# Another written order of the first and last steps of a four-layer graph-attention kernel, with 25 extra matmuls in the last batch

## The reference, cut to what matters

```
h = relu(layernorm(x)); x = x + L0(h)   # 4 heads of 64: softmax over adj of leaky(s_i + s_j), times h W; elu
h = relu(layernorm(x)); x = x + L1(h)   # MLP 256->512, full attention (no mask), elu + residual,
                                        # MLP 512->256, masked attention (W_hand), elu + residual, relu
h = relu(layernorm(x)); x = x + L2(h)   # masked attention with self loops (W2), elu
h = relu(layernorm(x)); x = x + L3(h)   # masked attention (W3), relu
```

## Time and profile before

| | |
|---|---|
| median of 3 runs (lowest, highest) | 3086.91 us (3084.91, 3088.44) |
| the profiled execution | 3088.44 us, of which its span is 3086.6 us |
| PE busy | 3027.8 us (98%) |
| DVE busy, ACT busy | 2453.4 us (79%), 2321.4 us (75%) |
| mean granted clock of TensorE | 0.996 of full speed (2.4 GHz) |
| chain that ended last | PE 82%, ACT 9%, DVE 7% |

### The profile page before, as it was taken

One profiled execution on the slowest core, in us unless ns is written; L12 is line 12 of the kernel. 1 busy time (PEld: TensorE's weight loads), 2 busy tenths in 40 slices (PEclk: granted clock), 3 DMA queues, 4 the chain that ended last, 5 costly groups with the idle time before them and its releaser, 6 DMA issues.

```text
span 3086.6 us, 58782 instructions
## 1 busy us (share of the span) xinstructions
PE 3027.8 (98%) x21528; PEld 2830.1 (92%) x21528; DVE 2453.4 (79%) x7049; ACT 2321.4 (75%) x6303; POOL 205.2 (7%) x410
## 2 busy tenths in 40 slices
PE   8999999999999999999999999999999999999998
PEld 7899999999999999999999999999999998999987
DVE  6878787887887888878878888888778787787866
ACT  6677777777778777778787787777787777877776
POOL 2000000000000000000000000000000000000000
PEclk9999999999999999999999999999999999999998
DMA  2000000000000000000000000000000000000000
GB/s 76 1 22 1 15 15 15 15 1 15 15 15 15 15 1 15 15 15 15 2 14 15 15 15 15 1 15 15 15 15 8 8 15 15 15 15 1 1 1 28
DMA packets 16336, 41.54 MB, mean 13 GB/s; under 512 B 5297, under 2 KB 6833, under 8 KB 16049
## 3 DMA queue, kind: packets, MB, share of 16 engines
q1 hardware_dynamic: 16048, 37.77, 3.5%
HBM read 20.99 MB, written 16.78 MB: 12 GB/s over the span
## 4 chain that ended last, share of the span: by engine, by line
PE 82%; ACT 9%; DVE 7%; issue 1%; POOL 1%; SPq 0%; DMA 0%; DVEq 0%; ACTq 0%
PE bank L516 45%; PE bank L585 14%; PE bank L620 14%; ACT Z L1044 4%; PE bank L573 4%; PE bank L537 2%; DVE R L792 2%; PE bank L671 2%; PE bank L561 1%; DVE x L1009 1%; DVE Z L1006 1%; ACT Z L1196 1%; ACT Z L1202 1%; ACT Z L1191 1%; ACT Z L1021 1%
## 5 line engine op out<-in xcount | busy, mean ns | idle before, releaser
L585 PE MATMUL bank<-hw,R 128*128 128x257 f32 x3072 | 707.4, 383 | 0.5 <-DVE R L792 0.5
L585 PEld LDWEIGHTS bank<-hw,R 128*128 128x128 f32 x3072 | 569.0, 191 | 75.5 <-ACT hw L1082 1.5
L620 PEld LDWEIGHTS bank<-hw,R 128*128 128x128 f32 x4096 | 490.9, 192 | 5.5 <-DVE hw L825 1.2
L620 PE MATMUL bank<-hw,R 128*128 128x65 f32 x4096 | 494.8, 270 | 0.8 <-DVE R L792 0.8
L792 DVE SCALAR_TENSOR_TENSOR R<-bank,E,mask_ne 128x512 f32<-128x512 f32 x640 | 450.5, 743 | 13.4 <-PE bank L573 12.5
L1044 ACT ACTIVATE Z<-x,nm,rs 128x256 f32<-128x256 f32 x512 | 283.2, 593 | 52.3 <-DVE x L1009 32.2
L1247 POOL TENSOR_TENSOR rs<-ve,mhalf 128x4 f32<-128x4 f32 x128 | 134.5, 1051 | 2825.7 <-DVE ve L744 2159.2
L516 PE MATMUL bank<-wfc_hi,oThi 128*128 128x256 f32 (+1 forms) x1024 | 302.0, 295 | 2.1 <-DVE oTlo L871 1.9
L516 PE MATMUL bank<-wfc_hi,oTlo 128*128 128x256 f32 (+1 forms) x1024 | 289.7, 283 | 0.0
L516 PE MATMUL bank<-wfc_lo,oThi 128*128 128x256 f32 (+1 forms) x1024 | 289.7, 283 | 0.0
L1067 ACT COPY Z<-bank 128x258 f32<-128x258 f32 (+1 forms) x512 | 183.1, 369 | 93.3 <-PE bank L516 93.0
(11 more groups left out here) (262 smaller groups left out, 8353.9 us busy)
## 6 DMA issues: line engine op xcount, KB each, us to landing
x<-in_x_dram SPq DMA_DIRECT2D x32, 512.0 KB, 3.4
out_dram<-x SPq DMA_DIRECT2D x32, 512.0 KB, 2.6
R<-in_adj_dram SPq DMA_DIRECT2D x2, 512.0 KB, 7.3
Z<-in_L_gnn_mlp_w_dram SPq DMA_DIRECT2D x2, 512.0 KB, 5.4
O<-in_L_gnn_W_fc_dram SPq DMA_DIRECT2D x1, 1024.0 KB, 6.7
R<-in_L_gnn_W_dram SPq DMA_DIRECT2D x1, 256.0 KB, 3.7
R<-in_L_gnn_W_hand_dram SPq DMA_DIRECT2D x1, 256.0 KB, 6.7
rowt<-in_L_gnn_W_dram SPq DMA_DIRECT2D x1, 256.0 KB, 4.7
```

The lines of the kernel that those rows point to most:

```text
L585: ins = e.matmul(bk[:, 0:257], P[:, j, i * 128:(i + 1) * 128], hw[:, j, 0:257], start=(j == 0), stop=(j == NBLK - 1))
L620: ins = e.matmul(bk[:, i * 66:i * 66 + 65], P[:, (4 * h + j) % PTILES, i * 128:(i + 1) * 128], hv[:, j, h, 0:65], start=(j == 0 and i == 0 ...
```

## The change

All ten start and end strings of `TURNS` but SP's start are written anew; the cycle strings stay, and so does the number of steps that each batch has behind it at the end of the start. `warm` gets a batch number, and in `turn(2)` and `turn(3)` of the last batch (31) it issues 10 and 15 matmuls of 512 columns ahead of the transposes, into the bank that these then overwrite.

```
-            def warm(bk, n):
-                if b == 0:
+            def warm(bk, n, only=0):
+                if b == only:
                     w.wait_ge(*at("hTlo", b, 0, 1))
                     for _ in range(n):
                         e.matmul(bk[:, :], W0["hi"][:, 0, 0:128], hT[s]["hi"][:, 0, :], start=True, stop=True)
...
                     bk = bank_of(b, f"hT{l}", k)
+                    if k == 0 and l > 1:
+                        warm(bk, (10, 15)[l - 2], B - 1)
                     for n in range(NBLK):
```

The strings, of which one line of PE's end stands here:

```
-         "0000011112112000000111101010001000011110011101001001111010100100000"),
+         "1000110000011000000010111010000000110000000000000000000000000000000"),
```

More of the change, by code:

```diff
@@ L69 @@
     "pe": (
-        ("wwww00ww0000000w00000ww00001w10w0000ww0000w1www111ww00ww00001000011w000w000w111100102000000000121001"
-         "1111002010000011111000000020202001100000112111211020100001102120100110002210101121111112122210102120"
-         "00211100211211102222110111110001001011011"),
+        ("wwww00w00000w000000w000ww0ww00ww000ww0w0w0w001www1w1w100w0000110100010000100121111000000000000100111"
+         "1100011000001111100000002000000101001112122211210012000101012101102002020200121112111111122201012100"
+         "00211210112111202222011111111000010001111"),
@@ L73 @@
         ("2221100111010010101102201122221020102110022222021211011110110111221100022112212101111020000121111112"
          "122212221111"),
[L75 to L79, removed]
-         "0000011112112000000111101010001000011110011101001001111010100100000"),
+        ("5554343444433344343455335555445345454455535353454444444443334343535445355334455434444435333544444544"
+         "5545545544344434422333322323232443244434343324234322444424333333342223332323342242324443344323333324"
+         "2224333433334443434334332332311222211122121332332332321132123231313133222223221222112112331212113323"
+         "2323212222131113222322223332323322221122200111100011010221022122112102112022220002201111111011010100"
+         "1221100022011120122011112002121111112221221211101011010000001101110101001001111110100000000000110011"
+         "1000110000011000000010111010000000110000000000000000000000000000000"),
@@ L81 @@
     ),
     "dve": (
[L83 to L86, removed]
+        ("wwwwwwwww0000ww0000000000000ww000w000w0000w00ww0w0w0w000001w10000w00110w1110000101011100100000000010"
+         "111000000w000101000100001100100000000111111000111111010100000010001000000022000101110212002112112210"
+         "2202120010201211201121101120100001020111111221211212010110112111111111211221200210112200002212122011"
+         "110000000"),
@@ L87 @@
         ("2122222221122202022111212201100001110221000020120012202211110211211222112201210201101010111111112211"
          "12111111111101000022201110022220010100211122122222"),
[L89 to L96, removed]
+        ("5455555555445535345454545534355344334343453535453545444454435453445345545435443534434443433443554544"
+         "3444443344443444435355444335553534343535344455455545443444444342444343243344233234432232223424223443"
+         "4423333324333332422434422442343343323332233223334324433333233333332342434332244242422332442334334443"
+         "4433333223331332123323323322112332221131131231332132222113222223233123132313221213121222221113222322"
+         "3122222222222211113313222131331311212311322223333233221222221222201210212122100122111120000201002211"
+         "2211021121111202120200012201112000011111011211102211110110100210111111202101120200220012102221111211"
+         "0011111111110111020101001102002011011011000001001010111010100010000000000111000000001000001001001111"
+         "000000001000000000000001000001100000100000100000000000001010000000"),
@@ L97 @@
     ),
     "act": (
-        ("wwwwwww0000w00www00w00wwww0wwww1wwww1101w11w0w00ww1www1ww1w0000w0000100www22w01002w000000w0020000000"
-         "0100020000002000010000101000200020101011020101000200000100101010002100001001100001001000111111100100"
-         "021010111101001100010112111010110000001101120112110001110101110100"),
+        ("wwwwwww0000w00ww0w000ww0wwwwwwwwwww01ww0ww0w11w1wwwwww01w12wwww0000w00120100011200100200000000000000"
+         "0010000000000000210001001000000000011110120010000001100100221000221100000021100001110100010111101200"
+         "000100111010101011010121110011100100110001120011121111000101010110"),
@@ L102 @@
         ("0200221112120112020221211021220222001122202112222122112121221212111220222122111122121211121211111202"
          "121212212221120222111011211112112122"),
[L104 to L111, removed]
+        ("3533554455443544353554544545553355334555535544455554544555445454454545545454354445545544455344454445"
+         "5445554545544535544434454544545443433355342442424423424243434334424442233244443442344443343434334433"
+         "3434244434433433334444323343433333444343443434433244324333443333334432232424313311122331313223323323"
+         "3333121121333323312332332233223233223223332332232132223332323223212222332332323233322313323221222322"
+         "2223121133132102200202122002211212122202201100222222011222211121122221211112222201121211222121101212"
+         "1111112122012212212112220221111112121210101100100111211101101101101112011110110011110001101011000101"
+         "1011110010000110110001100000011010011101001111000001100100000000000000010000000000000000010001000000"
+         "0000000000000000000000100000"),
@@ L112 @@
     ),
     "pool": (
-        ("wwwwww0wwwwwwwww1ww0w0w0"),
+        ("wwwwwwwwwwwwww0ww1w0ww00"),
         ("1222"),
-        ("45535444233312201010012"),
+        ("45535442433132201110020"),
     ),
@@ L120 @@
         ("21"),
-        ("54043221130"),
+        ("05144323210"),
     ),
```

## The result

| | before | after |
|---|---|---|
| median (lowest, highest) | 3086.82 us (3084.91, 3088.44) | 3111.23 us (3109.06, 3117.6) |
| profiled execution, its span | 3088.44, 3086.6 us | 3113.14, 3111.3 us |
| mean granted clock | 0.996 | 0.991 |

The ratio is 1.0088, with a 95% interval of 1.0068 to 1.0108, which is 21 to 33 us. I had forecast slower, by 8.4 us, in a range that ends at 3104: the direction is right, the size is three times what I summed, and outside the range.

The account below looks back on a forecast made before the run. PE, busy 98% of the span, was taken as the bound, with its losses at the ends. Tail +9.7, start +0.3 and form changes -1.6 gave +8.4 us: 3096.8 on the profiled execution, 3095.5 as median, range 3086 to 3104.

Parts of the forecast that it names:

- the lone chain: Tail from `31:m2k3` to PE's end: batch 31 nearly alone, its own serial steps summing to 72.6 us at full clock.
- the clock in the new tail: Half clock behind five thin patches of the new tail: 1.0 us each, 5.0 us slower (0 to 8.3).
- the stretch ahead of `31:m2k3`: PE's end lists before that step: 21.6 us of moved work, -3.9 and +1.0, so it starts at 3013.6.
- the start: New start lists: charges and credits sum to +0.3 us, kept as -7 to +5.
- The extra matmuls: 10 and 15 unread matmuls in batch 31's waits, 2.3 and 3.5 us: hidden, costing nothing.
- the rival of 3090.5: Tail: the extra matmuls hold the clock through all thin patches, the 5.0 us fall away; chance 0.17.
- the filled stop (-3.9): At `31:attf0.0`, seven steps of `30:att1b` fill the old stop, saving 2.56 us idle and half of 2.7 at half clock.
- 1.0 us of new waits: Ahead of `31:m2k3`: charge for new short waits in the denser stretch, 1.0 us (0 to 3).
- Both credits: Start: fillers reappearing ahead of `1:h1.0`, -2.7 us; batch 0's scores ahead of a mask step and `1:h0.2-3` filling a wait, -1.0.
- The charge at `0:att0b0`: Start, from `0:h2.3` to `0:att0b0`: the fillers `2:h0.1-3` go, +1.5 us.
- The +2.5 of the first charge: Start, around `0:hT1`: less filler ahead and one loading step left of three behind, +2.5 us.
- Fewer changes of form, -1.6: PE enters fp32r matmul runs 7 times less in the start, 9 in the end, 0.1 us each: -1.6 us.

Follow-up runs that it names:

- the attempt to hold the clock: New start on the old end of the kernel with 41 unread tail matmuls, plus 46 unread 256-column matmuls in six places of the start: 3085.82 us, ratio 1.0008.

## Why the prediction was right in direction and wrong in size

The mechanism that I named, the lone chain, is there and has the size that I summed. Three terms of the sum failed, each by some 5 us: the clock in the new tail, the stretch ahead of `31:m2k3`, and the start.

- **The lone chain: right.** 72.6 us summed, 72.5 measured once the clock is full, in two kernels. It is not luck in the sum: measured there, `31:m2k3` to `S0` takes 4.8 us (4.7 forecast), to `h2` 1.6 (1.6), to `row5` 5.4 (5.4), to the end of the attention 9.5 (9.3), to `h3` 11.3 (11.6), L2 15.0 (14.7), to `S1` 9.6 (9.9), L3 14.7 (14.7). The places that I named show in the waits: ahead of `h3`, `TM3`, `row6`, `S1`, `TM4`, `row7`. Ahead of `S0` the wait stands one step earlier, at `30:row7`.
- **The extra matmuls: right.** Hidden, with 1.19 and 1.96 us of idle time behind them, and no cost to be seen with and without them. They don't hold the clock, so the rival of 3090.5 falls.
- **"The clock in the new tail": mis-sized.** I took five stretches at 1.0 us, 5.0 in all, with a ceiling of 8.3. Measured: 82.8 - 72.5 = 10.3 us. I had given each patch the 3.3 us stretch of the earlier trace rows, though the same rows show one of 6.8. Where the work behind a patch is thin as well, the clock stays down: 6.7, 9.9 and 6.8 us. Little of it fell on waiting time: PE is busy for 25.9 of the 30.1 us, half of which is 13.0, and 10.3 of that is paid.
- **The stretch ahead of `31:m2k3`: mis-sized.** I had the filled stop (-3.9) against 1.0 us of new waits, so -2.9. Measured: 28.37 - 4.44 of the earlier part - 21.6 = +2.3. The stop at `31:attf0.0` is gone, as I said (six of the seven steps of `30:att1b` stand ahead of it, not seven); but 0.62 us at `29:row7`, 0.56 at `30:S0` and 1.87 in `31:h1.0` took its place, with two stretches at half clock, the first from 2945 on, the second the 3.2 us that begin at 2975.8 behind the stops of `31:h1.0`. In all PE idles only 0.5 us more than before over this part; the rest is clock. A stall filled in one place came back a step earlier. I had looked only for what waits behind that stop, not for what DVE delivers late ahead of it.
- **The start: mis-sized.** +0.3 summed, with nothing in it for the clock; 5.3 us at `1:att0b1` in the profiled execution. Both credits can be seen in PE's idle time: the 1.97 us ahead of and in `1:h1` are gone (-2.7 forecast), and ahead of batch 0's first scores and attention 0.9 us less is lost (-1.0). The charge at `0:att0b0` is 1.8 us (1.5 forecast), but behind it comes a stretch of 6.8 us at half clock.
  The +2.5 of the first charge came out as 3.6, and not ahead of `0:hT1`: from 52 to 59 us PE stops 0.7, 2.3 and 1.8 us, twice ahead of steps of loading that wait for ACT and once ahead of `1:h0.0` that waits for DVE. So the fillers themselves wait, and another stretch of 6.8 us at half clock lies there.
  From 40 us to the end of the start PE idles 9.35 us at a clock of 0.96, against 4.60 us at 0.99 over the same steps before; from the span's first instruction the difference in idle time is 3.3 us, and the rest of the 5.3 comes with two stretches of 6.8 us at half clock where there was one of 3.3 before. How exactly they divide, and whether the half clock makes some of the idle time, stays open, since the attempt to hold the clock did not hold it in the profiled execution.
- **Fewer changes of form, -1.6:** no run isolates it. The sum below is taken between anchors and would close with it or without it.

The sum by what was measured: 5.3 at the start, -0.8 given back by the cycle, 2.3 ahead of `31:m2k3`, and from there 82.8 - (86.5 - 21.6) = 17.9: 24.7 us. With the clock taken out of both tails the 17.9 are 12.7 of the lone chain and 10.3 - 5.1 = 5.2 of more half clock. My own term for this stretch was 12.7 as well (72.6 + 5.0 - 64.9), but that is a chance: it had 7.7 us of chain, since I held a chain at full clock against an old tail with its half clock in it, and 5.0 of clock. (In the last step of the forecast 3096.8 less 1.5 is 3095.3, not 3095.5; it changes nothing.)

"Perfetto Trace Analysis" of the Trainium skill, section "Optimization Strategy", which advises interleaving regimes with different bounds, is borne out: the old tail with two batches side by side loses 16.1 us, the new one 28.8. "TensorE: Matmul & The Clock Gate" of the Trainium skill has idle gaps throttle and dense work avoid it (section "HAM oscillation — how this bites in real kernels"): the trace agrees, since filling the waits brought the clock of the tail from 0.81 to 1.00. The longest gap in this tail was 2.5 us.

## What to carry to other kernels

When the order of a drain is judged, add up the last batch's serial chain twice: once at full clock, and once with every patch behind which PE stays thin at half clock for as long as the thin part lasts, not for one stretch each. Keep two batches side by side to the end, and look at what every engine delivers to the steps ahead of a filled stall before its gain is booked. Unread matmuls were worth having here only where they filled nearly all waits and fitted inside them: 25 in two places gave nothing measurable in the new order and cost 4 to 5 us in the old, 58 more in eleven places gave 10 in the tail, and 41 in the old order gave 4 to 5.

## What the runs showed of the hardware that I had not expected

- Half clock came back in stretches of very different length, with windows of 3.3, 6.7 to 6.8, 9.9 and 13.2 us wholly at half clock and one from 37 to 57.5 us in the start of the kernel with 46 fillings there, although no gap on PE was longer than 2.5 us in the tail of the changed kernel.
- Which of them occur varies between executions with the same order. The old start ran at half clock from 60 to 64 us in one kernel, from 86 to 93 in another and not at all in a third, unfilled in all three. In the tail the 2.56 us stop ahead of `31:attf0.0` is followed by half clock before (2968 to 2971.7) and in the kernel with the serial last layer, but not in the one with the extra matmuls alone, which has the same stop. So a price that is read from one execution is good to some us only: `1:att0b1` begins at 222.1 to 225.9 us in the seven profiled executions with the old start unfilled, and at 224.9 to 228.3 in the four with the new one, 3.2 us apart in the mean.
- In the old order 41 unread matmuls in the tail and 13 in the start were enough to keep the mean granted clock of a 3080 us kernel at 1.00 in the profiled execution, and the median fell by 5 us with PE doing more.
